# Bias vectors as one-partition rows spread by TensorE, and TensorE's repeated waits dropped, in a conditioned bottleneck adapter

## The chip, the cores and the metric

One core of one Trainium2 chip runs the kernel. The metric is the device time of one execution in microseconds (us); lower is better. The engines are named as in the profile: PE (TensorE), DVE (VectorE), ACT (ScalarE), POOL (GpSimd) and SP (SyncE, which here only issues DMAs).

## The reference

A bottleneck adapter whose two weight matrices depend on the batch. DIM = 512, BN = 128, H = 128; `x` is [4, 1024, 512], `cond` (the reference's `h_lang`) is [4, 128]; all is float32.

```python
dWd = ((h_lang @ Wdd.T + bdd) * DELTA_SCALE).reshape(B, BN, D)
dWu = ((h_lang @ Wdu.T + bdu) * DELTA_SCALE).reshape(B, D, BN)
Wd_b = Wd + dWd
Wu_b = Wu + dWu
down = jax.nn.relu(jnp.einsum('bld,bnd->bln', x, Wd_b) + bd)
up = jnp.einsum('bln,bdn->bld', down, Wu_b) + bu
return x + up
```

`Wdd` and `Wdu` are each [65536, 128], 33.5 MB; `x` and the output are 8.4 MB each; `bd` has 128 elements and `bu` 512.

## The kernel before, in words

**The stream of weights.** `Wdd` and `Wdu` come as 32 chunks of 1 MB each, 2048 rows to a chunk, 16 rows (8 KB) to a partition. SP issues all of them, in order, on its one DMA queue, into a ring of four buffers `w`. From the fifth chunk on each issue waits until DVE has transposed the chunk that held the buffer (`wt_ready`, L224). Between the chunks of the first turn SP issues the base weights: `base_d` and `bdd` after the second chunk (L253, L254), and after the fourth `Wu`, `bdu`, then `bu` as one row on partition 0 (`bu_row`, L259) and `bd` as one element on each of 128 partitions (`bd_col`, L260). Between the chunks of `Wdu` it issues eight pieces of `x` (L229). The stores of the output come last (L250).

**The work on a chunk.** DVE transposes it in blocks of 32x32 into the ring `wt` (L299; the last chunk in two parts, L356). PE sums each pair of chunks against `st`, the spread condition (L527, the last pair L644). After four chunks (a group) ACT copies the sums to `g_rows` (L372), and PE turns them (L538, L541 for `Wd`, L553 for `Wu`). For `Wd`, ACT copies the turned group into `wd_b` (L379). For `Wu`, ACT copies it (L405) and POOL adds its parts and the base into `wu_b` (L493, L496); for the last group DVE does that from PSUM (L310, L313).

**The work on x.** While `Wdu` streams, PE turns two blocks of rows of `x` (L607), ACT copies them to `xt` (L413), PE multiplies by `wd_b` (L617, function `down_unit`), and ACT applies the bias `bd_col` and the Relu (L421). POOL adds `bu_all` to `x` (L477). PE's product with `wu_b` (L634, function `up_unit`) is made in 32 units. The first 20 are copied by ACT (L430) and added to `x` by POOL (L484); the last 12 are added by DVE straight from PSUM (L341). The order of all units on each engine is written out by hand (`DOWN_AT`, `UP_COUNT`, `UNITS`). Four PSUM banks (`bank`) are used in turn; `wait_bank` waits for the earlier use.

**The work around the change.** In the first turn, after its seventh chunk, PE turns the base of `Wu` (L569) into `bank[1]` and spreads `bu_row` over all partitions with a product by a row of ones (L573) into `bank[2]`; ACT copies the two out (L390, L394). DVE adds `bdu` to `Wu` after its sixth chunk (L331), once all four loads of `base_u_loaded` are there. Before each unit PE waits for several semaphores: `down_unit` for `group_ready`, `x_copied` and `down_ready`; `up_unit` for `group_added`, for the last columns `last_added` too, for `down_ready`, and for its bank.

Of the kernel before, what the change touches and what calls it, by code (L numbers as in the profile page):

```python
# [37 lines left out]
I = L // P  # L38
# [67 lines left out]
def hyper_adapter(nc, x, cond, Wd, bd, Wu, bu, Wdd, bdd, Wdu, bdu, out):  # L106
# [10 lines left out]
    with ctx:  # L117
# [33 lines left out]

        bu_row, ones = up_s[0:1, 0, 0:D], up_s[0:1, 1, 0:P]

        gt_s = base_d[:].rearrange("p (c n) -> p c n", c=C)
# [5 lines left out]

        cond_loaded = sem("cond_loaded")
        base_d_loaded = sem("base_d_loaded")
        base_u_loaded = sem("base_u_loaded")
# [14 lines left out]
        ones_ready = sem("ones_ready")  # L178
        bu_spread = sem("bu_spread")
        bu_ready = sem("bu_ready")  # L180
        wt_ready = sem("wt_ready")
        pair_summed = sem("pair_summed")
# [38 lines left out]
        def _(sp):  # L221
# [34 lines left out]
            def load_base_u():  # L256
                sp.dma_start(wu_nat, Wu.rearrange("(d c) n -> d c n", c=C)).then_inc(base_u_loaded, 16)
                sp.dma_start(bdu_nat, bdu.rearrange("(d c n) -> d c n", c=C, n=N)).then_inc(base_u_loaded, 16)
                sp.dma_start(bu_row, bu.rearrange("(o d) -> o d", o=1)).then_inc(base_u_loaded, 16)  # L259
                sp.dma_start(bd_col[:], bd.rearrange("(p o) -> p o", o=1)).then_inc(base_u_loaded, 16)  # L260

# [16 lines left out]
        def _(dve):  # L278
# [36 lines left out]
            def turn(it):  # L315
                for u in range(TURN_CHUNKS):
# [11 lines left out]
                    if u == 5 and isinstance(it, int):  # L328

                        dve.wait_ge(base_u_loaded, 16 * 4)  # L330
                        nc.vector.scalar_tensor_tensor(wu_nat, bdu_nat, DELTA_SCALE, wu_nat,  # L331
                                                       ALU.mult, ALU.add).then_inc(base_u_summed, 1)
# [31 lines left out]
        def _(act):  # L364
            act.dma_start(cond_rows, cond.rearrange("b (r i) -> b r i", i=QUAD)).then_inc(cond_loaded, 16)

            def copy_group(g, n):
# [15 lines left out]
            def turn(it):  # L383
                for n in range(2):
# [3 lines left out]
                    if n == 1 and isinstance(it, int):  # L388
# [3 lines left out]
                                             ).then_inc(base_ready, 1)  # L392
                        act.wait_ge(bu_spread, 1)
                        nc.scalar.activation(bu_all[:], bank[2][:, 0:D], ACT.Copy).then_inc(bu_ready, 1)  # L394

            turn(0)
# [43 lines left out]
            copy_x_unit(1)  # L440
            act.wait_ge(base_u_loaded, 16 * 4)
            copy_down(0)
# [69 lines left out]
        def _(pe):  # L512
# [45 lines left out]
            def turn(it):  # L558
                for u in range(TURN_CHUNKS):
# [5 lines left out]
                    if u == 6 and isinstance(it, int):  # L565
# [4 lines left out]
                        last.then_inc(base_turned, 1)  # L570
                        pe.wait_ge(base_u_loaded, 16 * 4)
                        pe.wait_ge(ones_ready, 1)
                        nc.tensor.matmul(bank[2][:, 0:D], ones, bu_row, start=True, stop=True).then_inc(bu_spread, 1)  # L573
                    if u == 1 and not isinstance(it, int):
# [11 lines left out]
            def wait_bank(kind, n):  # L586

                use = USE_OF[kind, n] - BANK_RING
                if use < 0:
                    pe.wait_ge(base_ready, 1)  # L590
                    pe.wait_ge(bu_ready, 1)
                    return
                kind, n = BANK_USE[use]
# [17 lines left out]
            def down_unit(j):  # L611
                pe.wait_ge(group_ready, GROUPS)
                pe.wait_ge(x_copied, 2 * (j + 1))
                if j >= 1:
                    pe.wait_ge(down_ready, j)
# [5 lines left out]
            def turn_x_unit(j):  # L621
                turn_x(2 * j)
                turn_x(2 * j + 1)

            def up_unit(e):
                b, rows, cols = unit_at(e)
                pe.wait_ge(group_added, min(cols.stop * GROUPS // D, GROUPS - 1))
                if cols.stop == D:
                    pe.wait_ge(last_added, 1)
                pe.wait_ge(down_ready, (b * I + rows.stop) // UNIT_I)  # L630
                wait_bank("up", e)
# [74 lines left out]
```

## Time and profile before

| what | us |
|---|---|
| median of 3 runs | 213.4 |
| lowest, highest | 213.16, 213.97 |
| the profiled execution, its own time | 212.81 |
| span of its instructions and DMAs | 210.9 |
| outside the span (212.81 - 210.9) | 1.9 |
| PE busy | 168.1 |
| DVE busy | 159.9 |
| POOL busy | 74.1 |
| ACT busy | 57.5 |
| moved by DMA | 85.11 MB, mean 403 GB/s |

The table is of one execution, which was 0.6 us quicker than the median. A landing is the time at which the semaphore of a DMA has reached its count; it is seen as the start of the instruction that waited for it. A busy time says how long an engine had work, not that it set the time; the chain of waits says that. A DMA runs on up to 16 DMA engines, and it has landed when the last of them is done with its share.

### The profile page before, as it was taken

Reading aid. Unit: us, or ns where it says so; the run is one execution under the profiler, and the core shown is the slowest. Engines: PE = TensorE matmul, PEld = TensorE weight load, DVE = VectorE, ACT = ScalarE, POOL = GpSimd, SP = SyncE. Lnnn points to the kernel's source line nnn. Section 1 sums busy time; section 2 is a strip of 40 time slices with the busy share of each in tenths; the row PEclk is TensorE's granted clock in tenths of the full one; section 3 lists DMA queues with packets and bytes.
Section 4 is the critical chain, followed back from the end, with each engine's and each line's share of the span. In section 5 each row is a group of like instructions: output and inputs, shape, how many; then the busy total and the mean of one; then the engine's idle time right before and its main releaser. Section 6 shows DMA issues by size and latency. Waiting matters only on the chain.

```text
span 210.9 us, 3068 instructions
## 1 busy us (share of the span) xinstructions
PE 168.1 (80%) x1146; PEld 99.2 (47%) x1146; DVE 159.9 (76%) x88; ACT 57.5 (27%) x102; POOL 74.1 (35%) x58
## 2 busy tenths in 40 slices
PE   1066399677777673999895999999999999998980
PEld 0011153313324140476663767568666665557960
DVE  2866999899999999944744877458859999992770
ACT  2001014111111201053542454454444434543000
POOL 2000000000000000035843857599586578797000
PEclk9999999797969699799999999999999999999996
DMA  6999999999999999999999999999999999999997
GB/s 226 423 384 399 423 419 416 426 421 423 423 423 423 423 423 423 423 421 421 418 423 419 418 419 418 421 418 423 423 418 418 410 401 415 419 385 386 344 344 241
DMA packets 19510, 85.11 MB, mean 403 GB/s; under 512 B 1573, under 2 KB 9769, under 8 KB 10282
## 3 DMA queue, kind: packets, MB, share of 16 engines
q1 hardware_dynamic: 19490, 84.94, 99.2%
q8 instruction: 8, 0.13, 0.2%
q14 instruction: 4, 0.03, 0.0%
q10 hardware_dynamic: 8, 0.00, 0.0%
HBM read 76.55 MB, written 8.39 MB: 403 GB/s over the span
## 4 chain that ended last, share of the span: by engine, by line
DMA 65%; DVE 18%; PE 11%; issue 2%; SPq 0%; DVEq 0%
DMA w<-in_L_cond_Wdu_dram 35%; DMA w<-in_L_cond_Wdd_dram 30%; DVE wt L299 18%; PE bank L634 8%; PE acc L527 2%; PE acc L644 1%; PE gt L553 0%; SPq L225 0%; DVE xs L341 0%; DVE down L331 0%; DVEq L340 0%
## 5 line engine op out<-in xcount | busy, mean ns | idle before, releaser
L299 DVE STREAM_TRANSPOSE wt<-w 128x2048 f32<-128x2048 f32 x63 | 145.5, 2311 | 36.5 <-DMA w<-in_L_cond_Wdu_dram 25.9
L527 PE MATMUL acc<-wt,st 128*32 128x512 f32 x496 | 72.0, 706 | 33.4 <-DVE wt L299 33.0
L477 POOL TENSOR_TENSOR xs<-xs,bu_all 128x1024 f32<-128x1024 f32 x16 | 37.9, 2368 | 109.1 <-PE bank L607 109.1
L527 PEld LDWEIGHTS acc<-wt,st 128*32 128x32 f32 x496 | 14.7, 120 | 73.8 <-DVE wt L299 38.0
L634 PE MATMUL bank<-wu_b,down 128*128 128x128 f32 (+1 forms) x192 | 30.9, 313 | 0.5 <-issue 0.5
L617 PE MATMUL dn<-xt,wd_b 128*128 128x256 f32 x128 | 30.6, 382 | 0.0
L634 PEld LDWEIGHTS bank<-wu_b,down 128*128 128x128 f32 x192 | 26.5, 191 | 6.6 <-issue 4.5
L484 POOL TENSOR_TENSOR xs<-up_s,xs 128x512 f32<-128x512 f32 x20 | 25.2, 1278 | 5.0 <-ACT up_s L430 4.9
L617 PEld LDWEIGHTS dn<-xt,wd_b 128*128 128x128 f32 x128 | 23.0, 190 | 3.4 <-issue 0.8
L372 ACT ACTIVATE g_rows<-acc 128x512 f32<-128x512 f32 x16 | 9.6, 597 | 50.2 <-PE acc L527 48.7
L413 ACT ACTIVATE xt<-bank 128x512 f32<-128x512 f32 x32 | 17.4, 595 | 11.9 <-PE bank L607 11.9
L607 PEld LDWEIGHTS bank<-ident,xs 128*128 128x128 f32 x128 | 14.2, 141 | 8.9 <-issue 8.4
L607 PE MATMUL bank<-ident,xs 128*128 128x128 f32 x128 | 17.2, 277 | 0.0
L379 ACT ACTIVATE wd_b<-gt 128x256 f32 (+1 forms) x8 | 5.0, 626 | 40.8 <-PE gt L541 40.8
L430 ACT ACTIVATE up_s<-bank 128x512 f32<-128x512 f32 x20 | 11.9, 597 | 12.8 <-PE bank L634 10.2
L538 PEld LDWEIGHTS gt<-fold,g_rows 128*128 128x128 f32 x64 | 10.1, 199 | 7.1 <-issue 7.1
L538 PE MATMUL gt<-fold,g_rows 128*128 128x64 f32 x64 | 13.1, 288 | 0.0
L541 PE MATMUL gt<-ident,base_d 128*128 (+1 forms) x64 | 12.6, 280 | 0.0
L421 ACT ACTIVATE down<-dn,bd_col 128x256 f32<-128x256 f32 x16 | 7.6, 474 | 17.8 <-PE dn L617 17.8
L341 DVE TENSOR_TENSOR xs<-bank,xs 128x512 f32<-128x512 f32 x12 | 8.3, 692 | 3.3 <-PE bank L634 3.3
L541 PEld LDWEIGHTS gt<-ident,base_d 128*128 128x128 f32 x64 | 10.0, 197 | 0.0
L493 POOL TENSOR_TENSOR base_d<-base_d 128x256 f32<-128x256 f32 x7 | 5.1, 731 | 5.9 <-ACT base_d L405 5.9
(32 smaller groups left out, 35.5 us busy)
## 6 DMA issues: line engine op xcount, KB each, us to landing
w<-in_L_cond_Wdd_dram SPq DMA_DIRECT2D x32, 1024.0 KB, 7.4
w<-in_L_cond_Wdu_dram SPq DMA_DIRECT2D x32, 1024.0 KB, 10.1
xs<-in_x_dram SPq DMA_DIRECT2D x8, 1024.0 KB, 12.3
out_dram<-xs SPq DMA_DIRECT2D x4, 1024.0 KB, 10.8
out_dram<-xs SPq DMA_DIRECT2D x7, 512.0 KB, 5.6
out_dram<-xs SPq DMA_DIRECT2D x2, 256.0 KB, 4.9
base_d<-in_L_cond_Wd_dram SPq DMA_DIRECT2D x1, 256.0 KB, 7.1
down<-in_L_cond_bdd_dram SPq DMA_DIRECT2D x1, 256.0 KB, 7.3
```

The costliest lines, as they stand in the source:

```text
L299: nc.vector.transpose(wt[:, tslot].rearrange("p r (k j) -> p k r j", j=QUAD), w[:, slot, :].rearrange("p (k r h) -> p k r h", r=R, h=QUAD) ...
L372: nc.scalar.activation(g_rows[:, n].rearrange("p (j k) -> p j k", k=K), acc[n][:].rearrange("p (k j) -> p j k", k=K), ACT.Copy, scale=DELT ...
L413: nc.scalar.activation(xt[:, j % XT_RING, c0:c0 + BANK_C, :], bank_of("x", m)[:].rearrange("p (c l) -> p c l", c=BANK_C), ACT.Copy).then_i ...
L430: nc.scalar.activation(up_s[:, e % UP_RING], bank_of("up", e)[:], ACT.Copy).then_inc(up_copied, 1)
L477: nc.gpsimd.tensor_tensor(xs[:, b, i0:i0 + UNIT_I], xs[:, b, i0:i0 + UNIT_I], bu_pair, ALU.add).then_inc(bu_added, 1)
L484: nc.gpsimd.tensor_tensor(unit_x(e), unit_sums(e, up_s[:, e % UP_RING]), unit_x(e), ALU.add).then_inc(pool_final, 1)
L527: last = nc.tensor.matmul(a[TILE * place:TILE * (place + 1)], st[:, r, low * TILE:(low + 1) * TILE], wt[:, slot + h, r], start=low == 0 an ...
L538: nc.tensor.matmul(gt[:, k, 0:PART], g_rows[:, n, k * P:(k + 1) * P], fold[:], start=True, stop=False)
L541: last = nc.tensor.matmul(gt[:, k, 0:PART], base_d[:, k * P:(k + 1) * P], pick, start=False, stop=True)
L607: last = nc.tensor.transpose(bank_of("x", m)[:, n * P:(n + 1) * P], xs[:, b, i0 + i, c * P:(c + 1) * P], ident[:])
L617: last = nc.tensor.matmul(dn[:], wd_b[:, c, j // BATCH_UNITS], xt[:, j % XT_RING, c], start=c == 0, stop=c == C - 1)
L634: last = nc.tensor.matmul(place[:, n], down[:, b, i], wu_b[:, b, cols], start=True, stop=True)
```

## The change

`bu` and `bd` are both loaded as one row on partition 0, from ACT's queue and at the start of the kernel; `bd` was a load of one element to each of 128 partitions, on SP's queue. PE turns the row of `bd` into a column by a product with a single one, right behind the spread of `bu`, and ACT copies this column out of `bank[3]`. DVE waits for two loads in place of four. In `down_unit` and `up_unit` a wait for a count that PE has waited for earlier is left out. The ring, the chunks and the order of the units stay as they were.

```diff
@@ -150,6 +150,7 @@
         wu_nat, bdu_nat = nat[2], nat[3]
 
         bu_row, ones = up_s[0:1, 0, 0:D], up_s[0:1, 1, 0:P]
+        bd_row = up_s[0:1, 2, 0:N]
 
         gt_s = base_d[:].rearrange("p (c n) -> p c n", c=C)
 
@@ -159,6 +160,7 @@
         bank = [pb(f"bank{n}", [P, BANK_COLS]) for n in range(BANK_RING)]
 
         cond_loaded = sem("cond_loaded")
+        bias_loaded = sem("bias_loaded")
         base_d_loaded = sem("base_d_loaded")
         base_u_loaded = sem("base_u_loaded")
         w_loaded = [sem(f"w_loaded{n}") for n in range(W_RING)]
@@ -176,8 +178,9 @@
         base_turned = sem("base_turned")
         base_ready = sem("base_ready")
         ones_ready = sem("ones_ready")
-        bu_spread = sem("bu_spread")
+        bias_spread = sem("bias_spread")
         bu_ready = sem("bu_ready")
+        bd_ready = sem("bd_ready")
         wt_ready = sem("wt_ready")
         pair_summed = sem("pair_summed")
         g_ready = sem("g_ready")
@@ -256,8 +259,6 @@
             def load_base_u():
                 sp.dma_start(wu_nat, Wu.rearrange("(d c) n -> d c n", c=C)).then_inc(base_u_loaded, 16)
                 sp.dma_start(bdu_nat, bdu.rearrange("(d c n) -> d c n", c=C, n=N)).then_inc(base_u_loaded, 16)
-                sp.dma_start(bu_row, bu.rearrange("(o d) -> o d", o=1)).then_inc(base_u_loaded, 16)
-                sp.dma_start(bd_col[:], bd.rearrange("(p o) -> p o", o=1)).then_inc(base_u_loaded, 16)
 
             turn(0)
             with sp.Fori(1, TURNS) as it:
@@ -327,7 +328,7 @@
                                                        ALU.mult, ALU.add).then_inc(base_d_summed, 1)
                     if u == 5 and isinstance(it, int):
 
-                        dve.wait_ge(base_u_loaded, 16 * 4)
+                        dve.wait_ge(base_u_loaded, 16 * 2)
                         nc.vector.scalar_tensor_tensor(wu_nat, bdu_nat, DELTA_SCALE, wu_nat,
                                                        ALU.mult, ALU.add).then_inc(base_u_summed, 1)
 
@@ -363,6 +364,8 @@
         @block.scalar
         def _(act):
             act.dma_start(cond_rows, cond.rearrange("b (r i) -> b r i", i=QUAD)).then_inc(cond_loaded, 16)
+            act.dma_start(bu_row, bu.rearrange("(o d) -> o d", o=1)).then_inc(bias_loaded, 16)
+            act.dma_start(bd_row, bd.rearrange("(o n) -> o n", o=1)).then_inc(bias_loaded, 16)
 
             def copy_group(g, n):
 
@@ -390,8 +393,9 @@
                         nc.scalar.activation(base_u[:].rearrange("n (d c) -> n c d", c=C),
                                              bank[1][:].rearrange("n (c d) -> n c d", c=C), ACT.Copy
                                              ).then_inc(base_ready, 1)
-                        act.wait_ge(bu_spread, 1)
+                        act.wait_ge(bias_spread, 1)
                         nc.scalar.activation(bu_all[:], bank[2][:, 0:D], ACT.Copy).then_inc(bu_ready, 1)
+                        nc.scalar.activation(bd_col[:], bank[3][:, 0:1], ACT.Copy).then_inc(bd_ready, 1)
 
             turn(0)
             with act.Fori(1, TURNS) as it:
@@ -438,7 +442,7 @@
             copy_x_unit(0)
             store_group(GROUPS - 1)
             copy_x_unit(1)
-            act.wait_ge(base_u_loaded, 16 * 4)
+            act.wait_ge(bd_ready, 1)
             copy_down(0)
             for t in range(CHUNKS - PAIR):
                 if t % SLOTS == 2:
@@ -568,9 +572,11 @@
                         for k in range(C):
                             last = nc.tensor.transpose(bank[1][:, k * P:(k + 1) * P], wu_nat[:, k], ident[:])
                         last.then_inc(base_turned, 1)
-                        pe.wait_ge(base_u_loaded, 16 * 4)
+                        pe.wait_ge(bias_loaded, 16 * 2)
                         pe.wait_ge(ones_ready, 1)
-                        nc.tensor.matmul(bank[2][:, 0:D], ones, bu_row, start=True, stop=True).then_inc(bu_spread, 1)
+                        nc.tensor.matmul(bank[2][:, 0:D], ones, bu_row, start=True, stop=True)
+                        nc.tensor.matmul(bank[3][:, 0:1], bd_row, ones[:, 0:1], start=True, stop=True
+                                         ).then_inc(bias_spread, 1)
                     if u == 1 and not isinstance(it, int):
                         turn_down_group(2 * it - 1, 1)
                     if u == SLOTS + 1:
@@ -589,6 +595,7 @@
                 if use < 0:
                     pe.wait_ge(base_ready, 1)
                     pe.wait_ge(bu_ready, 1)
+                    pe.wait_ge(bd_ready, 1)
                     return
                 kind, n = BANK_USE[use]
                 if kind == "x":
@@ -609,8 +616,9 @@
                 last.then_inc(x_turned, 1)
 
             def down_unit(j):
-                pe.wait_ge(group_ready, GROUPS)
                 pe.wait_ge(x_copied, 2 * (j + 1))
+                if j == 0:
+                    pe.wait_ge(group_ready, GROUPS)
                 if j >= 1:
                     pe.wait_ge(down_ready, j)
                 for c in range(C):
@@ -622,12 +630,19 @@
                 turn_x(2 * j)
                 turn_x(2 * j + 1)
 
+            def downs_for(e):
+                b, rows, _ = unit_at(e)
+                return (b * I + rows.stop) // UNIT_I
+
             def up_unit(e):
+
                 b, rows, cols = unit_at(e)
-                pe.wait_ge(group_added, min(cols.stop * GROUPS // D, GROUPS - 1))
-                if cols.stop == D:
-                    pe.wait_ge(last_added, 1)
-                pe.wait_ge(down_ready, (b * I + rows.stop) // UNIT_I)
+                if e == 0 or cols.stop > unit_at(e - 1)[2].stop:
+                    pe.wait_ge(group_added, min(cols.stop * GROUPS // D, GROUPS - 1))
+                    if cols.stop == D:
+                        pe.wait_ge(last_added, 1)
+                if downs_for(e) > max([downs_for(before) for before in range(e)], default=0):
+                    pe.wait_ge(down_ready, downs_for(e))
                 wait_bank("up", e)
                 place = unit_sums(e, bank_of("up", e)[:])
                 for n, i in enumerate(range(rows.start, rows.stop)):
```

## Rows read from the trace of the kernel before

**Rows 1.** the page's 40 slices of the span: DMA engines busy in tenths, GB/s
```profile
DMA  6999999999999999999999999999999999999997
GB/s 226 423 384 399 423 419 416 426 421 423 423 423 423 423 423 423 423 421 421 418 423 419 418 419 418 421 418 423 423 418 418 410 401 415 419 385 386 344 344 241
```

**Rows 2.** the chain of work that ended last; start us, length us, what
```profile
1.21 6.92 DMA w<-in_L_cond_Wdd_dram
...
10.50 11.56 DMA w<-in_L_cond_Wdd_dram
...
60.00 7.45 DMA w<-in_L_cond_Wdd_dram
...
170.07 7.52 DMA w<-in_L_cond_Wdu_dram
...
179.98 1.92 PE acc L527 x16
...
193.98 10.73 PE bank L634 x64
...
204.81 0.69 DVE xs L341
```

**Rows 3.** the waits by engine and line; total us, times, longest us
```profile
DVE wt L299 <- DMA w<-in_L_cond_Wdu_dram: 25.9, 29, 2.7
```

**Rows 4.** the timeline of DVE, 8 to 24 us; start, length, instruction, idle before
```profile
11.99 2.31 DVE L299 STREAM_TRANSPOSE wt<-w 128x2048 f32<-128x2048 f32 x1 [1.52 <-DMA w<-in_L_cond_Wdd_dram]
14.48 2.31 DVE L299 STREAM_TRANSPOSE wt<-w 128x2048 f32<-128x2048 f32 x1 [0.18 <-DMA w<-in_L_cond_Wdd_dram]
...
19.60 2.31 DVE L299 STREAM_TRANSPOSE wt<-w 128x2048 f32<-128x2048 f32 x1 [2.09 <-DMA w<-in_L_cond_Wdd_dram]
```

**Rows 5.** busy time by stretch, cut at landings; last are granted clock, DMA share, GB/s
```profile
8.13:11.97 3.84, 1.35 (x8) 0.46 (x12) 2.31 (x1) 0.00 (x0) 0.00 (x0) 1.00 1.05 436
11.97:14.46 2.49, 2.29 (x12) 0.23 (x4) 2.31 (x1) 0.00 (x0) 0.00 (x0) 1.00 0.97 396
14.46:19.58 5.12, 2.73 (x16) 0.59 (x16) 3.02 (x3) 0.00 (x0) 0.00 (x0) 1.00 0.96 373
```

**Rows 6.** the DMA view of 15 to 17 us, in slices of 0.05 us
```profile
DMA  1999928009949305970594993003997459993903
...
DMA packets 210, 0.58 MB, mean 291 GB/s; under 512 B 121, under 2 KB 121, under 8 KB 145
```

**Rows 7.** the DMA issues of SP and ACT in the first 30 us
```profile
0.75 0.55 ACTq L365 DMA_DIRECT2D xt<-in_cond_dram  x1
...
5.47 0.35 SPq L260 DMA_DIRECT2D bd_col<-in_L_cond_bd_dram  x1
...
8.05 21.84 SPq L225 DMA_DIRECT2D w<-in_L_cond_Wdd_dram  x8
```

**Rows 8.** the timeline of 31 to 46 us, around the spread of bu
```profile
33.02 1.12 PE L573 MATMUL bank<-up_s 1*128 1x512 f32 x2
...
34.38 1.92 PE L527 MATMUL acc<-wt,st 128*32 128x512 f32 x16 [0.24 <-DVE wt L299]
34.49 2.31 DVE L299 STREAM_TRANSPOSE wt<-w 128x2048 f32<-128x2048 f32 x1 [0.17 <-DMA w<-in_L_cond_Wdd_dram]
34.67 0.59 ACT L372 ACTIVATE g_rows<-acc 128x512 f32<-128x512 f32 x1
...
36.23 0.43 PE L538 MATMUL gt<-fold,g_rows 128*128 128x64 f32 x2
...
37.64 2.31 DVE L299 STREAM_TRANSPOSE wt<-w 128x2048 f32<-128x2048 f32 x1 [0.84 <-DMA w<-in_L_cond_Wdd_dram]
```

**Rows 9.** the page's groups of matmuls of the two units; last, PE's idle time before
```profile
L634 PE MATMUL bank<-wu_b,down 128*128 128x128 f32 (+1 forms) x192 | 30.9, 313 | 0.5 <-issue 0.5
L617 PE MATMUL dn<-xt,wd_b 128*128 128x256 f32 x128 | 30.6, 382 | 0.0
```

**Rows 10.** the timeline of DVE from 184 us, its last step before the last units
```profile
193.25 0.63 DVE L313 TENSOR_TENSOR wu_b<-gt,wu_b 128x256 f32<-128x256 f32 x1
```

## The prediction

> **What bounds the kernel now.** I read the slices first. The DMA engines show a 9 from the second slice to the last but one, at about 420 GB/s in most slices until 155 us, and 241 to 386 GB/s in the last five, where stores are in the mix [rows 1]. So the kernel is a stream of loads with work hung on it. The chain of waits says the same: it goes from one landing of `w` to the next until 177.6 us (170.07 + 7.52), then over one transpose to PE at 179.98, and stays on PE until 204.7 (193.98 + 10.73); the last add of DVE ends at 205.5, and 5.4 us of store follow to the end of the span at 210.9 [rows 2]. An issue lands 7.45 us later, three chunks' time, so the queue is never empty [rows 2]. DVE is not the bound: in the second half it waited 29 times for a chunk of `Wdu` [rows 3]. What is to be seen: time that a load costs in the stream before 180 us comes back at the end one for one, if PE, DVE and ACT can follow. They can, as their own starts hang on the landings: a saving made near 20 us moves all of them alike.
>
> One place in the stream stands out. Between two landings with nothing else in between lie 2.49 us, the second stretch of [rows 5]. Between the landings at 8.13 and 11.97 lie one chunk and two base loads of 256 KB, the same bytes as between 14.46 and 19.58 but for 2.5 KB. The first takes 3.84 us, the second 5.12 [rows 4, 5]. The second is the one with `bu` and `bd` in it. The DMA view of 15 to 17 us shows it: 121 packets under 512 B, and slices of 0.05 us in which the 16 engines stand still; DMA moves 291 GB/s there [rows 6].
>
> **What the change removes.** The excess of the second interval is 5.12 - 3.84 = 1.28 us. That is the time that the latest of the 16 engines lost, since a chunk has landed when the last share is in. The engines together lost less: 8.13 to 14.46 us moves 436 x 3.84 + 396 x 2.49 = 2660 KB in 6.33 us, 420 GB/s; 14.46 to 19.58 moves at 373 GB/s [rows 5], so (420 - 373) x 5.12 / 420 = 0.57 us are lost on the average engine. The other 0.7 us are a lag of one engine behind its neighbours. How much of the lag is there at the end depends on which engine is late by then. Later lateness falls on single engines too: between the transposes at 34.49 and 37.64 lie 3.15 us in place of 2.49, a loss of 0.66 that the stream keeps [rows 8]. If that hits another engine than the one that `bd` held up, then that engine sets the landings before and after the change, and the change gives back what `bd` cost this engine: about the average. If it is always the same one, the whole 1.28 come back. No row tells the engines apart. I take 0.7 us, near the average, as there are 16 engines and only one is the latest of them at 19.58; the bounds are 0.3 (an engine that `bd` hurt half as much as the average) and 1.28.
>
> **What the change adds at the start.** ACT issues two more DMAs behind `cond`, about 0.55 us each [rows 7]. ACT's first work after them is the copy of the first group, which needs four chunks, and the fourth lands at 14.46 [rows 4]; nothing waits. SP saves two issues of about 0.35 us, and gains nothing: its next issue waits for a transpose until 8.05 [rows 7]. The rows are 2 KB and 0.5 KB. A chunk puts 64 KB on each engine in 2.49 us [rows 5], so 2.5 KB on one engine cost 0.10 us, of which 0.08 (`bu`) were there before. Term: +0.02, between 0 and +0.66, if the row stalls one engine as at 37.64 [rows 8].
>
> The Trainium skill ("DMA: Bandwidth & Descriptors", section "Issuing engines are not separate DMA queues") says that a DMA issued by another engine runs on the same 16 DMA engines and saves only the time of issue. The trace of before can't show that for `bd`; taken alone it would make the move to ACT's queue worth nothing, and leave the gain to the shape of the load.
>
> **What it adds at 33 us.** PE gets one more product behind the spread of `bu`. The spread's two instructions take 1.12 us for 512 columns, ending at 34.14, and PE then idles 0.24 us before its next pair at 34.38 [rows 8]. One column costs at most 0.3 us, cheaper than these, so the pair starts 0.06 us late at worst. ACT copies one column more: between 0.2 and 0.6 us (the 512-column copy), I take 0.35. The copy of the next group, 34.67 to 35.26, ends 0.35 later at 35.6, and the product that reads it starts at 36.23 behind PE's pair [rows 8]: cover 0.97 us. Without it, 0.35 us would fall on PE, which is not on the chain there. DVE and the stream see nothing of either. Term: 0.
>
> `down`'s activation reads the bias from the new column; it comes in the second half of the stream, long after the copy. DVE's wait for two loads in place of four is for loads that landed before 19.58. Term: 0.
>
> **What the dropped waits are worth.** 15 waits for `group_ready`, 28 for `group_added`, 11 for `last_added` and 20 for `down_ready` go, 74 in all. They could save time only where PE stands idle for them. Before the 128 matmuls of `down_unit` PE idled 0.0 us, before the 192 of `up_unit` 0.5 us in all [rows 9]; these 0.5 are the wait before 193.98, which is a real one, for DVE's sum that ends at 193.88 (193.25 + 0.63) [rows 2, 10]. From there PE needs 0.10 us to its first matmul, with two further waits in between of which one goes. Term: -0.03 us, between 0 and -0.10 at this place. In the run of 64 behind it there is no idle to be saved.
>
> **The sum.** -0.7 + 0.02 + 0 - 0.03 = -0.7 us. The profiled execution is 210.9 of span and 1.9 around it, 212.8; it would be 212.1. The runs shown have their median at 213.4, 0.6 above it; the same step gives **212.7 us**, 0.3% less.
>
> **The rivals.**
>
> A, the forecast: `bd` out of the stream returns 0.3 to 1.05 us, for 212.3 to 213.1.
>
> B, all of it comes back: the engine held up by `bd` is the one that sets the landings to the end, and 1.28 + 0.03 return: 212.1 or less, faster by over 0.5%. For it: the landing at 19.58 itself must come 1.28 earlier, and the transposes follow 0.02 us behind. Against it: the lateness at 37.64, on an engine of its own.
>
> C, nothing comes back: the stall at 15 to 16.5 us belongs to `Wu` and `bdu`, or another engine's lateness has covered it by the end; then 213.3 to 213.5. Against it: `base_d` and `bdd` have the same size, and their interval has no such loss [rows 5]. The Trainium skill gives (same page, section "Bandwidth", measured for another kind of issue) some 10.5 ns for a packet. By that, an estimate, 128 packets over 16 engines are 8 x 10.5 ns = 0.08 us, and the change would give 213.3. The rows show the 0.57 to 1.28 us, so I give the case little.
>
> D, slower: the one-partition rows stall one engine. It happens if they, among the first packets of the first chunk, hold up one engine as at 37.64, by 0.66 us each, while the engine that sets the landings had lost only 0.3 to `bd`: 1.32 - 0.3 = +1.0, 214.4. It decides against the change from a stall of 0.7 us on. For it: each row is one packet on one engine, and the stream keeps what one engine loses. Against it: `bu` is such a row already, and no more than a part of 1.28 can be its doing.
>
> **How the numbers follow.** A 0.55, B 0.25, C 0.15, D 0.05. 0.5% is 1.07 us, about what a measurement of this kernel can tell from no change. B gives faster, and the upper edge of A with the spread of the runs (0.8 us between the three) a little: faster 0.29. A and C give the same: 0.65. D, with some of C: slower 0.06. The range takes in A, most of B (down to -1.5, with both bounds of the small terms) and C: 211.9 to 213.4.
>
> **What would show it.** Right: no packet burst under 512 B near 15 us; the transpose of the fifth chunk starts at 18.3 to 18.9 in place of 19.60; PE's last run of 64 starts 0.3 to 1.1 us before 193.98 and is still 10.7 us long; the same number of matmuls but for two. Wrong: an interval near 5.1 us between the fourth and fifth landing (case C), a second landing later than 8.13 (case D), or a fifth landing early and a last one not, which would be lateness of another engine. I would also be wrong if PE's last stretch from 179.98 to 193.98 shrinks by more than 0.1 us: then the waits were worth more than I read.

## The result and the profile after

| | before | after |
|---|---|---|
| median of 6 runs each | 213.28 us | 211.5 us |
| lowest, highest | 212.6, 213.97 | 211.23, 211.94 |
| ratio of after to before, 95% interval | | 0.992 (0.9897 to 0.9943) |
| the profiled execution, span | 212.81, 210.9 | 211.89, 210.1 |

The change made the kernel 0.8% faster, where I had forecast 0.3% and a range that ended at 211.9. The changed kernel was timed twice more, on two different chips: 0.9919 (0.9889 to 0.9949) and 0.9941 (0.9917 to 0.9964). Over all comparisons the kernel before had a median of 213.1 us (114 runs, 212.0 to 215.7; three above 400 us are left out), and the kernels with both biases loaded as rows one of 211.8 (52 runs of the change, of its loads alone and of the rows on SP's queue; 211.1 to 212.7). By these the gain is 1.35 us (0.6%), and 1.8 was on the high side of it.

The page of the changed kernel, in slices of the span; the third and fourth slice (10.5 to 21 us) now read 412 and 421 GB/s, where they read 384 and 399 [rows 1]:

```profile
DMA  6999999999999999999999999999999999999997
GB/s 223 425 412 421 424 423 420 420 424 423 421 416 424 423 423 420 423 426 418 421 421 421 416 418 423 418 424 420 424 420 423 423 420 420 415 384 384 315 338 249
```

The stretches between the same four landings (us, then busy time of the five engines, granted clock, DMA share, GB/s):

```profile
8.24:12.07 3.83, 1.35 (x8) 0.46 (x12) 2.31 (x1) 0.00 (x0) 0.00 (x0) 1.00 1.05 437
12.07:14.56 2.49, 2.29 (x12) 0.22 (x4) 2.31 (x1) 0.00 (x0) 0.00 (x0) 1.00 0.97 396
14.56:18.39 3.83, 1.44 (x8) 0.40 (x12) 3.02 (x3) 0.00 (x0) 0.00 (x0) 1.00 1.05 429
```

The third stretch is now 3.83 us, as long as the first, which holds the same bytes; it was 5.12 [rows 5]. The DMA view of 15 to 17 us has 12 packets under 512 B in place of 121, 431 GB/s in place of 291, and only one empty slice [rows 6]:

```profile
DMA  9799949389973979937909794939497937997937
...
DMA packets 133, 0.86 MB, mean 431 GB/s; under 512 B 12, under 2 KB 12, under 8 KB 33
```

The transposes by which the saving can be followed, first in the kernel before, then in the changed one (start, length, what, idle time before and what ended it). They are those of the fifth chunk (before: [rows 4]), the thirteenth, the 35th, the 36th and the last (there are 64, 32 of each matrix):

```profile
40.22 4.70 DVE L299 STREAM_TRANSPOSE wt<-w 128x2048 f32<-128x2048 f32 x2 [0.28 <-DMA w<-in_L_cond_Wdd_dram]
```

```profile
99.75 2.31 DVE L299 STREAM_TRANSPOSE wt<-w 128x2048 f32<-128x2048 f32 x1 [2.65 <-DMA w<-in_L_cond_Wdu_dram]
103.15 2.31 DVE L299 STREAM_TRANSPOSE wt<-w 128x2048 f32<-128x2048 f32 x1 [1.08 <-DMA w<-in_L_cond_Wdu_dram]
```

```profile
187.52 2.37 DVE L356 STREAM_TRANSPOSE wt<-w 128x1024 f32<-128x1024 f32 x2
```

```profile
18.41 2.31 DVE L300 STREAM_TRANSPOSE wt<-w 128x2048 f32<-128x2048 f32 x1 [0.81 <-DMA w<-in_L_cond_Wdd_dram]
...
39.61 2.31 DVE L300 STREAM_TRANSPOSE wt<-w 128x2048 f32<-128x2048 f32 x1 [0.28 <-DMA w<-in_L_cond_Wdd_dram]
```

```profile
99.16 2.31 DVE L300 STREAM_TRANSPOSE wt<-w 128x2048 f32<-128x2048 f32 x1 [2.66 <-DMA w<-in_L_cond_Wdu_dram]
101.64 2.31 DVE L300 STREAM_TRANSPOSE wt<-w 128x2048 f32<-128x2048 f32 x1 [0.17 <-DMA w<-in_L_cond_Wdu_dram]
```

```profile
186.19 2.37 DVE L357 STREAM_TRANSPOSE wt<-w 128x1024 f32<-128x1024 f32 x2 [0.16 <-DMA w<-in_L_cond_Wdu_dram]
```

The fifth starts 1.19 us earlier (18.41 for 19.60), the thirteenth 0.61, the 35th 0.59, the 36th 1.51, the last 1.33. So the saving shrank and came back. Both changes stand beside a fetch of code: the one packet on the instruction queue in the kernel before between 34.5 and 36 us, then the one between 100.5 and 103.2 (queue, kind, packets, MB, share of 16 engines):

```profile
q8 instruction: 1, 0.02, 4.4%
```

```profile
q8 instruction: 1, 0.02, 2.5%
```

4.4% of 16 x 1.5 us are 1.06 us, on one engine, for 16 KB; the other is 2.5% of 16 x 2.7 = 1.08. Beside the first, both kernels lost time, and the changed one more. At the second the kernel before lost 0.92 us (3.40 between its 35th and 36th transpose, 2.48 in the changed one). But this second loss belongs to one execution: the second profile of the kernel before (experiment 5) has the same fetch between 100.5 and 103.2 us, and its 36th transpose comes 2.48 us behind its 35th:

```profile
99.74 2.31 DVE L299 STREAM_TRANSPOSE wt<-w 128x2048 f32<-128x2048 f32 x1 [2.66 <-DMA w<-in_L_cond_Wdu_dram]
102.22 2.31 DVE L299 STREAM_TRANSPOSE wt<-w 128x2048 f32<-128x2048 f32 x1 [0.17 <-DMA w<-in_L_cond_Wdu_dram]
```

In this pair of executions the stream kept all that the load had cost; that it did so by way of the fetches is argued from their place in time, and no run tests it.

The chain of the changed kernel shows why the span fell by 0.8 only and not by 1.3:

```profile
1.21 7.02 DMA w<-in_L_cond_Wdd_dram
...
96.53 12.54 DMA w<-in_L_cond_Wdu_dram
...
109.09 2.32 DVE wt L300
...
111.55 3.52 PE acc L531 x16
...
120.44 1.85 PE acc L531 x16
...
188.45 1.86 PE acc L659 x32
...
193.26 10.73 PE bank L649 x64
...
204.09 0.69 DVE xs L342
```

From 111.55 us it is on PE, until DVE's last add. There 16 matmuls took 3.52 us that took 1.92 in the first profile of the kernel before, at 112.89 us, and the stretch of it had a granted clock of 0.54, close to the lower of the two levels, 1.2 of 2.4 GHz; PE had stood idle in the stretch before:

```profile
110.00:111.50 1.50, 0.00 (x0) 0.00 (x0) 1.41 (x1) 0.00 (x0) 1.41 (x2) 0.97 0.97 404
111.50:115.10 3.60, 3.55 (x17) 0.79 (x18) 1.03 (x1) 0.00 (x0) 0.05 (x1) 0.54 1.02 423
115.10:120.00 4.90, 4.90 (x31) 4.49 (x32) 4.46 (x3) 2.61 (x5) 3.59 (x2) 1.00 1.02 423
```

PE was 1.6 us late from then on, and in the chain it waits for no chunk again. The last run of 64 starts 7.07 us behind the last transpose (186.19 to 193.26), in the profile of before 6.46 (187.52 to 193.98). Its length is the same, 10.7 us. This is no feature of the change: one more profile of the change has 6.48, and a second one of the kernel before has 6.83, with the same slow burst:

```profile
112.23 3.48 PE L527 MATMUL acc<-wt,st 128*32 128x512 f32 x16 [2.43 <-DVE wt L299]
```

There too the chain is on PE from 112.23 us. Such bursts are not rare earlier on: each profile has seven to eleven between 10 and 92 us, this one for instance in the first profile of the kernel before, in a stretch with a granted clock of 0.55. What is special at 112 us is that PE has little idle time behind it in which to catch up: in the changed kernel 0.5 us in all, before its last run.

```profile
40.00 3.40 PE L527 MATMUL acc<-wt,st 128*32 128x512 f32 x16 [1.77 <-DVE wt L299]
```

At 31 us the new product and the new copy are seen; the copy of the next group starts 0.05 us after the start of the new one:

```profile
30.86 1.12 PE L577 MATMUL bank<-up_s 1*128 1x512 f32 x2
...
31.82 0.27 PE L578 MATMUL bank<-up_s 1*128 1x1 f32 x2
...
32.13 0.60 ACT L397 ACTIVATE bu_all<-bank 128x512 f32<-128x512 f32 x1
32.62 0.17 ACT L398 ACTIVATE bd_col<-bank 128x1 f32<-128x1 f32 x1
32.67 0.60 ACT L375 ACTIVATE g_rows<-acc 128x512 f32<-128x512 f32 x1
```

### The profile page after: what moved, and what is told of

It is laid out like the page before. It is cut to its first block, busy times and chain, and to the rows that moved or that the text cites. A ratio compares the mean times of both kernels' runs of the same rounds, so it can differ in the third digit from the quotient of the medians.

```text
span 210.1 us, 3048 instructions
## 1 busy us (share of the span) xinstructions
PE 169.7 (81%) x1148; PEld 100.7 (48%) x1148; DVE 159.9 (76%) x88; ACT 57.6 (27%) x103; POOL 74.1 (35%) x58
## 4 chain that ended last, share of the span: by engine, by line
PE 44%; DMA 41%; DVE 11%; issue 1%; SPq 0%; DVEq 0%
DMA w<-in_L_cond_Wdd_dram 30%; PE bank L649 14%; PE acc L531 12%; DVE wt L300 11%; DMA w<-in_L_cond_Wdu_dram 11%; PE dn L625 10%; PE bank L614 5%; PE gt L557 1%; PE acc L659 1%; SPq L228 0%; DVE xs L342 0%; DVEq L341 0%
## 5 line engine op out<-in xcount | busy, mean ns | idle before, releaser
L531 PE MATMUL acc<-wt,st 128*32 128x512 f32 x496 | 73.2, 719 | 31.1 <-DVE wt L300 31.1
L542 PEld LDWEIGHTS gt<-fold,g_rows 128*128 128x128 f32 x64 | 10.6, 208 | 9.1 <-issue 9.1
L542 PE MATMUL gt<-fold,g_rows 128*128 128x64 f32 x64 | 13.7, 298 | 0.0
L545 PE MATMUL gt<-ident,base_d 128*128 (+1 forms) x64 | 13.4, 293 | 0.0
L545 PEld LDWEIGHTS gt<-ident,base_d 128*128 128x128 f32 x64 | 10.7, 210 | 0.0
```

The costliest lines, as they stand in the source:

```text
L531: last = nc.tensor.matmul(a[TILE * place:TILE * (place + 1)], st[:, r, low * TILE:(low + 1) * TILE], wt[:, slot + h, r], start=low == 0 an ...
L542: nc.tensor.matmul(gt[:, k, 0:PART], g_rows[:, n, k * P:(k + 1) * P], fold[:], start=True, stop=False)
L545: last = nc.tensor.matmul(gt[:, k, 0:PART], base_d[:, k * P:(k + 1) * P], pick, start=False, stop=True)
```

## The experiments

In the shortened edits `extra` is a tile that nothing reads, with its own semaphore, on which only the end of the kernel waits. The interval named is that between the starts of the fourth and the fifth transpose, in us: 5.12 in the first profile of the kernel before, 3.83 in the changed kernel.

**1. The parts of the change.** The loads alone (the change with PE's waits as before):

```diff
             def down_unit(j):
+                pe.wait_ge(group_ready, GROUPS)
                 pe.wait_ge(x_copied, 2 * (j + 1))
-                if j == 0:
-                    pe.wait_ge(group_ready, GROUPS)
...
             def up_unit(e):
-                if e == 0 or cols.stop > unit_at(e - 1)[2].stop:
-                    pe.wait_ge(group_added, min(cols.stop * GROUPS // D, GROUPS - 1))
-                    if cols.stop == D:
-                        pe.wait_ge(last_added, 1)
-                if downs_for(e) > max([downs_for(before) for before in range(e)], default=0):
-                    pe.wait_ge(down_ready, downs_for(e))
+                pe.wait_ge(group_added, min(cols.stop * GROUPS // D, GROUPS - 1))
+                if cols.stop == D:
+                    pe.wait_ge(last_added, 1)
+                pe.wait_ge(down_ready, (b * I + rows.stop) // UNIT_I)
```

> The changed kernel with PE's waits as in the kernel before: only the bias loads and their spread are changed. Theory S (stream): the column load of bd in the stream cost its full 1.3 us, and the waits are worth nothing: 211.6 to 212.0, as the changed kernel, fifth transpose near 18.4 us. Theory W (waits): once the stream is quicker PE sets the end, and the dropped waits gave the part beyond 1.3 us: this kernel comes at 212.0 to 212.6.

Measured: 211.6 us, ratio 0.9905 (0.9869 to 0.9941). The loads alone are as fast as the change, within what these runs can tell. The waits alone are the reverse of this edit, made in the kernel before:

> The kernel before with only PE's repeated waits dropped. Theory S: no change, 213.2 to 213.4, as the stream sets PE's starts and PE has no idle before its units. Theory W: 0.3 to 0.8 us faster, 212.5 to 213.0.

Measured: 212.84 us, ratio 0.9969 (0.9942 to 0.9996). That is 0.5 us, in the range of the theory that I did not hold, so both parts were run again, with the whole change beside them on one chip.

> The changed kernel with PE's waits as before, once more, beside the other part and the whole on one chip. If the waits are worth nothing: equal to the whole change within 0.2 us, 1.3 to 1.8 us below the kernel before. If they are worth 0.5 us in themselves: 0.5 us above the whole change.

> The kernel before with only the waits dropped, once more. If the waits are worth nothing: equal to the kernel before within 0.3 us. If they are worth 0.5 us: 0.4 to 0.6 us below it.

> The whole change, the base for the two parts on this chip: 211.4 to 212.0 us.

Measured: loads alone 211.91 us, 0.994 (0.9917 to 0.9964); waits alone 212.79, 0.9987 (0.9961 to 1.0013); the whole 211.83, 0.9941 (0.9917 to 0.9964). Beside the loads the waits are worth 0.1 us both times (211.6 to 211.5, 211.91 to 211.83), less than these runs can tell from nothing. Alone they are worth 0.3 to 0.5, once with an interval that excludes no change and once with one that includes it. The kernel of experiment 4 with one column added, which also has the waits dropped, stands at 0.9967 (0.9941 to 0.9992), as the waits alone did the first time. So two of three such kernels are just clear of the kernel before; whether the waits do something while the column is in the stream stays open.

**2. Place or shape.** The column, as before, but with `bu` at the start of ACT's queue:

```diff
-                sp.dma_start(bu_row, bu.rearrange("(o d) -> o d", o=1)).then_inc(base_u_loaded, 16)
-                sp.dma_start(bd_col[:], bd.rearrange("(p o) -> p o", o=1)).then_inc(base_u_loaded, 16)
...
+            act.dma_start(bu_row, bu.rearrange("(o d) -> o d", o=1)).then_inc(bias_loaded, 16)
+            act.dma_start(bd_col[:], bd.rearrange("(p o) -> p o", o=1)).then_inc(bias_loaded, 16)
```

> The kernel before with both bias loads moved to the start of ACT's queue, bd still as one element to each of 128 partitions, waits as before. Theory shape (the 128 small packets hold up the engines wherever they lie): the loss moves to the first chunk, which lands about 1 us later than at 5.7, and the time is 213.0 to 213.5. Theory place (it costs only behind the 2 KB packets of the base loads, or in a full stream; early it falls into the time in which the first packets are fetched): 211.7 to 212.2.

Measured: 213.38 us, 1.0005 (0.9976 to 1.0034). The loss has moved with the load. The first five transposes:

```profile
5.77 2.31 DVE L298 STREAM_TRANSPOSE wt<-w 128x2048 f32<-128x2048 f32 x1 [1.55 <-DMA w<-in_L_cond_Wdd_dram]
9.21 2.31 DVE L298 STREAM_TRANSPOSE wt<-w 128x2048 f32<-128x2048 f32 x1 [1.13 <-DMA w<-in_L_cond_Wdd_dram]
13.35 2.31 DVE L298 STREAM_TRANSPOSE wt<-w 128x2048 f32<-128x2048 f32 x1 [1.83 <-DMA w<-in_L_cond_Wdd_dram]
15.83 2.31 DVE L298 STREAM_TRANSPOSE wt<-w 128x2048 f32<-128x2048 f32 x1 [0.17 <-DMA w<-in_L_cond_Wdd_dram]
...
19.66 2.31 DVE L298 STREAM_TRANSPOSE wt<-w 128x2048 f32<-128x2048 f32 x1 [0.81 <-DMA w<-in_L_cond_Wdd_dram]
```

The first is where it was, where I had expected the loss; the second lies 3.44 us behind it in place of 2.45 to 2.58, and the third 1.36 us later than before; the fourth to the fifth is 3.83, and the fifth is where it was before. The other way round, both rows in the old place on SP's queue:

```diff
-            act.dma_start(bu_row, bu.rearrange("(o d) -> o d", o=1)).then_inc(bias_loaded, 16)
-            act.dma_start(bd_row, bd.rearrange("(o n) -> o n", o=1)).then_inc(bias_loaded, 16)
...
                 sp.dma_start(bdu_nat, bdu.rearrange("(d c n) -> d c n", c=C, n=N)).then_inc(base_u_loaded, 16)
+                sp.dma_start(bu_row, bu.rearrange("(o d) -> o d", o=1)).then_inc(bias_loaded, 16)
+                sp.dma_start(bd_row, bd.rearrange("(o n) -> o n", o=1)).then_inc(bias_loaded, 16)
```

> The changed kernel, waits dropped, with both rows issued by SP in the old place behind the base loads of Wu. Theory shape: 211.4 to 211.8, as the changed kernel, and the interval between the fourth and fifth landing is 3.8 to 3.9 us. Theory place: the interval stays above 4.5 us and the time is 212.5 to 213.3.

Measured: 211.46 us, 0.9896 (0.986 to 0.9932), and the interval is 3.82:

```profile
14.48 2.31 DVE L302 STREAM_TRANSPOSE wt<-w 128x2048 f32<-128x2048 f32 x1 [0.19 <-DMA w<-in_L_cond_Wdd_dram]
...
18.30 2.31 DVE L302 STREAM_TRANSPOSE wt<-w 128x2048 f32<-128x2048 f32 x1 [0.81 <-DMA w<-in_L_cond_Wdd_dram]
```

So the saving goes with the shape of the load of `bd`; the queue and the two places tried make no difference that these runs can tell.

**3. No load of bd.**

```diff
-                sp.dma_start(bd_col[:], bd.rearrange("(p o) -> p o", o=1)).then_inc(base_u_loaded, 16)
...
+            nc.gpsimd.memset(bd_col[:], 0.0).then_inc(bd_zeroed, 1)
```

> The kernel before without any load of bd; the bias of the down product is zero, so this part of the computation is left out. It measures what the column load costs in all. If the load is the whole gain of the change: 211.3 to 211.8. If half of the gain is from elsewhere (the move of bu, the waits): 212.1 to 212.6.

Measured: 212.2 us, 0.9939 (0.9916 to 0.9963), interval 3.83. The stream has the whole saving at the fifth transpose. The time lies in my second range, in which half of the gain comes from elsewhere. The changed kernel itself was not timed beside it; two kernels that were, the change with a cheap load added (64 and 512 bytes, experiment 4), stand at 212.1 and 212.0, no lower. So the time does not show that the missing load gives less than the row, nor does it rule it out.

**4. Doses and sizes.** Each of these adds a load to the changed kernel, behind `bdu` on SP's queue. One column of 4 bytes, and two:

```diff
+                sp.dma_start(extra[:, 0, 0:1], bd.rearrange("(p o) -> p o", o=1)).then_inc(extra_loaded, 16)
```

> The changed kernel with one column load of bd (128 packets of 4 bytes) added in the old place, into a tile that nothing reads. Theory S: it gives back all of the gain, 213.0 to 213.5, interval between fourth and fifth landing 4.5 to 5.6 us. If the way through the one-partition row were part of the gain: 212.2 to 212.8.

> The changed kernel with two column loads of bd (128 packets of 4 bytes each) added to SP's queue in the old place, into a tile that nothing reads. If a column load costs its price each time: fifth landing 2.5 us later than in the changed kernel, time 213.5 to 215. If the engines pay once for a switch to small packets: 212.8 to 213.4.

Measured: one, 212.66 us, 0.9967 (0.9941 to 0.9992), beside 211.88 for the change on that chip; two, 213.99 us, 1.0027 (1.0 to 1.0054). The fourth and fifth transposes with one, then with two:

```profile
14.50 2.31 DVE L304 STREAM_TRANSPOSE wt<-w 128x2048 f32<-128x2048 f32 x1 [0.19 <-DMA w<-in_L_cond_Wdd_dram]
...
19.74 2.31 DVE L304 STREAM_TRANSPOSE wt<-w 128x2048 f32<-128x2048 f32 x1 [2.22 <-DMA w<-in_L_cond_Wdd_dram]
```

```profile
14.74 2.31 DVE L305 STREAM_TRANSPOSE wt<-w 128x2048 f32<-128x2048 f32 x1 [0.19 <-DMA w<-in_L_cond_Wdd_dram]
...
21.15 2.31 DVE L305 STREAM_TRANSPOSE wt<-w 128x2048 f32<-128x2048 f32 x1 [3.39 <-DMA w<-in_L_cond_Wdd_dram]
```

5.24 and 6.41 us: 1.41 and 2.58 over the 3.83 without. Each load pays its price. In the stream the one is as Theory S has it (4.5 to 5.6). In time it is not: 212.66 lies in the range of the second theory (212.2 to 212.8), as the column gave back 0.7 to 0.8 of the 1.3 us that separate the two kernels on that chip. That the way through the row is a part of the gain is still unlikely, as the kernel without any load of `bd` (experiment 3) has the same interval as the rows; where the rest of the time went stays open. The profiled execution, at 213.24, was one of its slowest.

64 bytes and 512 bytes to each of the 128 partitions, from rows 2 KB apart:

```diff
+                sp.dma_start(extra[:, 0, 0:16], Wd[:, 0:16]).then_inc(extra_loaded, 16)
```

```diff
+                sp.dma_start(extra[:, 0, 0:128], Wd[:, 0:128]).then_inc(extra_loaded, 16)
```

> The changed kernel with one load of 64 bytes to each of 128 partitions added in the old place, into a tile that nothing reads. If what costs is a packet below 512 bytes: 212.8 to 213.4, as with 4 bytes. If the price falls with the size: 211.6 to 212.4.

> The changed kernel with one load of 512 bytes to each of 128 partitions added in the old place, into a tile that nothing reads. Its 64 KB are a sixteenth of a chunk, 0.16 us of the stream. If the number of packets costs: 212.8 to 213.4. If only packets below 512 bytes are dear: 211.6 to 211.9, and the interval between fourth and fifth landing is 4.0 us.

Measured: 212.09 us, 0.9947 (0.9921 to 0.9972), and 212.03 us, 0.9943 (0.9921 to 0.9966). The intervals are 3.91 and 4.06, so 64 bytes cost 0.08 us and 512 cost 0.23. With 64 bytes:

```profile
14.54 2.31 DVE L304 STREAM_TRANSPOSE wt<-w 128x2048 f32<-128x2048 f32 x1 [0.18 <-DMA w<-in_L_cond_Wdd_dram]
...
18.45 2.31 DVE L304 STREAM_TRANSPOSE wt<-w 128x2048 f32<-128x2048 f32 x1 [0.89 <-DMA w<-in_L_cond_Wdd_dram]
```

So it was neither the number of packets nor their being under 512 bytes. Two things were still mixed: 4 bytes came from neighbouring addresses, 64 from addresses 2 KB apart. The two missing corners:

```diff
+                sp.dma_start(extra[:, 0, 0:1], Wd[:, 0:1], allow_slow_non_contiguous=True).then_inc(extra_loaded, 16)
```

```diff
+                sp.dma_start(extra[:, 0, 0:16], bdd[0:2048].rearrange("(p o) -> p o", o=16)).then_inc(extra_loaded, 16)
```

> As the one with 4 bytes to each of 128 partitions, but the 128 sources lie 2 KB apart in DRAM (the first column of Wd). Theory packet (a write of 4 bytes to a partition is what is dear): 213.0 to 213.5, as with neighbours. Theory source (128 reads of the same few lines of DRAM are what is dear): 211.6 to 212.2.

> The changed kernel with 64 bytes to each of 128 partitions added in the old place, the sources lying side by side (8 KB of bdd). Theory packet: 211.8 to 212.3, as with 64 bytes from 2 KB apart. Theory source: dearer than that by some tenths, 212.3 to 213.0, as the 128 reads again fall into one small stretch of DRAM.

> The changed kernel itself, as the base of the three beside it: 211.4 to 212.0. Its fifth landing should again lie 3.8 us behind the fourth, and PE's last run of 64 should start near 192.7 us where no matmuls at half clock fall into the second half, 193.3 where they do.

Measured: the change itself 211.88 us, 0.9919 (0.9889 to 0.9949). 4 bytes from 2 KB apart: 211.85 us, 0.9906 (0.9868 to 0.9945). 64 bytes side by side: 211.9, 0.9923 (0.9893 to 0.9954). Neither costs anything that can be timed. In the profile of the change itself PE's last run started at 193.03, with no slow burst in the second half, where I had expected 192.7. The transposes with 4 bytes from 2 KB apart, 3.91 us:

```profile
14.47 2.31 DVE L304 STREAM_TRANSPOSE wt<-w 128x2048 f32<-128x2048 f32 x1 [0.18 <-DMA w<-in_L_cond_Wdd_dram]
...
18.38 2.31 DVE L304 STREAM_TRANSPOSE wt<-w 128x2048 f32<-128x2048 f32 x1 [0.89 <-DMA w<-in_L_cond_Wdd_dram]
```

The DMA view of 14.5 to 17 us, first with 4 bytes from neighbouring addresses, then with 4 bytes from 2 KB apart:

```profile
DMA  9998999995357090960439630696909899597695
...
DMA packets 328, 0.70 MB, mean 279 GB/s; under 512 B 165, under 2 KB 165, under 8 KB 269
```

```profile
DMA  9999998799999939939399393996939939399693
...
DMA packets 370, 1.03 MB, mean 413 GB/s; under 512 B 166, under 2 KB 166, under 8 KB 270
```

Nearly the same number of small packets, 165 and 166, and 279 against 413 GB/s. So the column of `bd` is not dear because its packets are small or many; what is left of the things varied is that its 128 reads go to one stretch of 512 bytes of DRAM. Neighbouring 4-byte reads were made from `bd` alone: whether another vector of that kind costs the same, or the place of `bd` in DRAM has a part in it, was not tried.

**5. A second profile of the kernel before.**

> The kernel before, for a second profile of it. If the price of the column load varies between executions: an interval between fourth and fifth landing other than 5.12 us by some tenths, anywhere from 4.4 to 6. If it is fixed: 5.1.

Measured: 213.16 us, interval 5.06. The four profiles with one column in its old place have 5.12 and 5.06 (kernel before), 4.46 and 5.08 (waits alone), so the price was 0.6 to 1.3 us in them. The whole table, from the timelines of DVE and PE:

```
column of 4 B in its place or added       4th to 5th   last transpose   last run of PE
before                                       5.12         187.52            193.98
before, again                                5.06         187.17            194.00
waits alone                                  4.46         187.41            193.85
waits alone, again                           5.08         187.20            193.65
change + 4 B from neighbours                 5.24         188.21            194.67
no such column
after                                        3.83         186.19            193.26
change, again / third                        3.84 / 3.84  186.55 / 186.67   193.03 / 193.47
loads alone / again                          3.83 / 3.82  186.28 / 186.31   192.76 / 193.27
rows on SP's queue                           3.82         186.74            194.04
no load of bd                                3.83         186.22            192.66
```

The last transposes have means of 187.50 and 186.42, 1.08 apart, and PE's last runs 194.03 and 193.21, 0.82 apart. The fifth row is the changed kernel with a load added; without it the last transposes are 0.90 apart. For these four profiles with the column in its old place and the seven without it, the mean saving along the stream, from the timelines of DVE, is 1.08 us at the fifth transpose, 0.53 at the 13th, 0.50 at the 35th, 0.98 at the 43rd and 0.90 at the last chunk. So, in the means, about half of it was hidden from the 12th chunk to the 35th, and most of that came back behind the 36th.

The last run of PE depends on one thing more. Without a slow burst near 112 us it starts 6.4 to 6.5 us behind the last transpose, and there the column makes 1.0 us: 193.98, 193.85 and 193.65 with it in its old place, 193.03, 192.76 and 192.66 without. In the profiles with a slow burst it starts 81.6 to 81.8 us behind that burst, in either kernel: 194.00 with the column (one profile), 193.26 to 194.04 without (four).

## Why the prediction was wrong, point by point

**The bound.** Right for the profile that I had: there the stream of loads set the end, and a saving near 20 us came out at the end. That PE can follow in every case was wrong: PE is nearly the bound itself, before the change too (second profile of the kernel before), so that one burst at the lower clock near 112 us puts the chain on PE.

**What the change removes.** This is the step that failed, by the size of its term, -0.7 us. I saw the excess of 1.28 us and its place, and then took 0.7, as the average engine had lost only 0.57 and later lateness might fall on another engine. Measured: the interval fell by 1.29 (5.12 to 3.83), the last transpose by 1.33 in the pair of profiles and by 0.9 to 1.1 in the means, the time by 1.35 over all runs and by 1.8 in the first comparison. What I argued from exists: from the 12th chunk to the 35th only 0.5 us of the saving is left. But it did not last to the end of the stream. Why it came back between the 36th and the 43rd transpose is not known, and no row tells the engines apart, so that the rule that I took, the average engine's loss, is neither explained nor replaced by another. What came back in time was about the price of the landing, 1.28, and not the mean over the engines: the outcome of rival B, to which I gave 0.25.

The signs that I named for my forecast did appear in the profile: the fifth transpose at 18.41, PE's last run 0.72 us earlier and 10.7 us long, PE's matmuls 1148 for 1146, and the profiled execution 0.92 us shorter, inside the 0.3 to 1.05 of rival A. These signs could not tell A from B, as a slow burst of PE took 0.6 us of the 1.33 there. It was the step from the profiled executions to the median of all runs, taken as the same for both kernels, that the profiles do not bear out: seven profiled executions without the column lie on average 0.8 us below the four with it in its old place, where all runs are 1.35 apart. In the first comparison the profiled execution of the kernel before lay 0.5 below its median, and that of the changed kernel 0.4 above.

**The size of the gain beyond 1.29.** In the first comparison it was 1.8 us. Of the 114 runs of the kernel before 17 lie more than 1 us above their median, up to 215.7; of the 52 with rows none does. That fits a price that is at times above 1.3, but no execution of that kind was profiled, and the cause of these runs stays open.

**The start.** Right: the first transposes stand within 0.1 us of where they were (8.26 for 8.16, 12.09 for 11.99), ACT issues its two rows in 0.23 and 0.27 us, half of my 0.55, and nothing waits for them:

```profile
1.33 0.23 ACTq L367 DMA_DIRECT2D up_s<-in_L_cond_bu_dram  x1
1.59 0.27 ACTq L368 DMA_DIRECT2D up_s<-in_L_cond_bd_dram  x1
```

Rival D, a row that stalls one engine at the start, did not come; the column does something of that kind there, at the second and third chunk (experiment 2).

**At 33 us.** Right in effect. The one-column product takes 0.27 us, the copy 0.17 in place of my 0.35, and the next copy starts 0.05 us after it has started.

**The waits.** 0.03 us forecast; 0.1 measured beside the loads, within the noise. PE idles 0.5 us before `up_unit`'s matmuls after as before.

**Rival C** is out: the loss was `bd`'s, 1.29 us of it. The Trainium skill ("DMA: Bandwidth & Descriptors", section "Bandwidth") gets its 10.5 ns by dividing the 0.67 us of a small transfer by its 64 packets. I divided by the 16 engines once more. Read as a price for each packet of the transfer, an estimate, 128 packets are 1.34 us: near the 1.41 measured for neighbouring addresses, but not what the same number of packets from addresses 2 KB apart cost, 0.08 (3.91 - 3.83). By neither reading does one price for a packet fit both. The same page ("Specifications") puts the smallest transfer at full rate at 512 bytes. The runs agree in so far as 8 KB in packets of 64 bytes cost 0.08 us, 102 GB/s, and 64 KB in packets of 512 cost 0.23 us, 285 GB/s; both are below the stream's 420. The small packets are slow for their bytes, but with so few bytes they cost little. Its rule that the issuing engine makes no difference (section "Issuing engines are not separate DMA queues") agrees with experiment 2 (211.46 on SP's queue, 211.5 on ACT's).

## What to carry to other kernels

In a kernel that streams without a gap, compare intervals between landings that hold the same bytes; an interval that is too long is the price of what lies in it. How much of it comes back at the end has to be measured: here the delay of the landing was 1.3 us, the loss of the average engine 0.57, and the time gained 1.35 over all runs, though the stream had only 0.5 of it in its middle. Load a short vector as one row and turn it into a column on TensorE when it has to go one element to a partition; here the queue made no difference. Waits for counts already reached gave nothing that could be told from noise once the column was gone, in a kernel whose PE had no idle time before them. And a range taken from one profile of each kernel is too narrow for a gain of 1 us: take several, and see whether PE or the stream ends each of them.

## What the runs showed of the hardware that was not expected

128 reads of 4 bytes from one stretch of 512 bytes of DRAM (`bd`) held the stream up by 1.2 to 1.4 us in most profiles (0.6 in one), at both places tried and each time anew (2.58 for two). 128 packets of 4 bytes with sources 2 KB apart cost 0.08 us, and 64 bytes side by side (8 KB in all) 0.07.

A fetch of 16 KB of code kept one DMA engine for 1.06 to 1.08 us. The chunk that landed beside it came 0.9 us late in one profile of the kernel before and on time in the other; that the fetch was the cause is not shown.

PE's 16 matmuls of a pair took 3.52 us in place of 1.92 at a granted clock of 0.54, right behind an idle stretch from 110 to 111.5 us; it happened in some executions of either kernel, between 111.5 and 113.2 us, in each of them after PE had waited over 2 us for DVE. Such a wait did not always bring it: in the first profile of the kernel before PE had waited 2.27 us at 112.89 and the 16 matmuls took 1.92 us.
